# Seven half-depth products (Strassen) for queries, keys and gates of a linear-attention layer, over two halves of the tokens

## What is computed

```
h = layernorm(x)
qkv = silu(h @ qkv_w.T)            # 32 heads of 128; q, k, v per head
gate = sigmoid(h @ gate_w.T)       # 2048 x 4096
attn = causal linear attention with a decay per head (64 tokens, as one masked product)
y = gate * norm_w * rms_normalised(attn over all 4096)
x = x + y @ out_w.T
x = x + cross attention with ctx_4096 (64 channels, softmax over 512)
x = x + layernorm(x) @ identity.T
```

## Time and profile before

| | us |
|---|---|
| median of three runs | 2329.49 (2328.81 to 2329.71) |
| profiled execution | 2330.04 |
| its span, first to last instruction | 2328.2 |
| TensorE busy | 2291.6 (98%) |
| VectorE busy | 1208.5 (52%) |
| ScalarE busy | 732.1 (31%) |
| GpSimd busy | 442.3 (19%) |

### The profile page before, as it was taken

How to read it: one execution, slowest core, us unless ns; L and a number is a source line. 1 busy time by engine, 2 the same in 40 slices (tenths; PEclk the granted TensorE clock), 3 DMA queues, 4 the chain that set the end, 5 groups by cost and what they waited for, 6 DMA issues and landing times. The chain is left out here.

```text
span 2328.2 us, 34076 instructions
## 1 busy us (share of the span) xinstructions
PE 2291.6 (98%) x14112; PEld 1896.4 (81%) x14112; DVE 1208.5 (52%) x1493; ACT 732.1 (31%) x1303; POOL 442.3 (19%) x394
## 2 busy tenths in 40 slices
PE   8999999999999999999999999999999999799998
PEld 6888888888888888888888888888888888555555
DVE  6653545454444545454545454545444454576765
ACT  3232222232222222232323232223222222466664
POOL 2311122222211222222211122222211122211110
PEclk9999999999999999999999999999999999899999
DMA  4010100000000001010101000000000000201000
GB/s 138 1 47 1 38 8 28 18 28 18 28 18 19 27 0 46 0 46 0 46 0 46 0 28 18 28 18 28 18 28 18 18 23 1 104 19 34 31 24 19
DMA packets 24046, 61.75 MB, mean 27 GB/s; under 512 B 2880, under 2 KB 5440, under 8 KB 23872
## 3 DMA queue, kind: packets, MB, share of 16 engines
q1 hardware_dynamic: 24000, 61.11, 7.6%
HBM read 56.90 MB, written 4.19 MB: 26 GB/s over the span
## 5 line engine op out<-in xcount | busy, mean ns | idle before, releaser
L444 PE MATMUL bank<-xn_hi,w_hi 128*128 128x512 f32 x1536 | 612.2, 399 | 2.9 <-DVE w_lo L327 2.9
L446 PE MATMUL bank<-xn_hi,w_lo 128*128 128x512 f32 x1536 | 599.6, 390 | 0.0
L445 PE MATMUL bank<-xn_lo,w_hi 128*128 128x512 f32 x1536 | 599.2, 390 | 0.0
L220 POOL TENSOR_TENSOR sq<-attn 128x512 f32<-128x512 f32 x128 | 179.0, 1398 | 1527.8 <-ACT attn L289 1517.0
L444 PEld LDWEIGHTS bank<-xn_hi,w_hi 128*128 128x128 f32 x1536 | 288.9, 188 | 63.8 <-issue 3.2
L446 PEld LDWEIGHTS bank<-xn_hi,w_lo 128*128 128x128 f32 x1536 | 288.8, 188 | 61.6
L445 PEld LDWEIGHTS bank<-xn_lo,w_hi 128*128 128x128 f32 x1536 | 289.2, 188 | 55.6
L489 PE MATMUL bank<-w_hi,xn_lo 128*128 128x256 f32 x1024 | 289.2, 282 | 0.0
L487 PE MATMUL bank<-w_hi,xn_hi 128*128 128x256 f32 x1024 | 289.2, 282 | 0.0
L488 PE MATMUL bank<-w_lo,xn_hi 128*128 128x256 f32 x1024 | 289.0, 282 | 0.0
L363 DVE TENSOR_TENSOR qk<-bank,qk 128x512 f32<-128x512 f32 x256 | 174.0, 690 | 218.9 <-ACT qk L253 216.8
(11 more groups left out here) (89 smaller groups left out, 2709.5 us busy)
## 6 DMA issues: line engine op xcount, KB each, us to landing
raw<-w_qkv SPq DMA_DIRECT2D x48, 512.0 KB, 3.7
raw<-w_gate SPq DMA_DIRECT2D x16, 512.0 KB, 4.4
raw<-w_out SPq DMA_DIRECT2D x16, 512.0 KB, 3.2
stage<-ctx_in SPq DMA_DIRECT2D x16, 256.0 KB, 2.8
xr<-x SPq DMA_DIRECT2D x4, 1024.0 KB, 11.2
out<-attn_acc SPq DMA_DIRECT2D x16, 256.0 KB, 2.0
attn_acc<-x SPq DMA_DIRECT2D x3, 1024.0 KB, 7.8
attn_acc<-x SPq DMA_DIRECT2D x4, 256.0 KB, 3.9
```

Of the source, the lines that this page charges most:

```text
L220: nc.gpsimd.tensor_tensor(sq[:, :], attn[:, h], attn[:, h], ALU.mult).then_inc(sq_made, 1)
L444: nc.tensor.matmul(dst, hi, xn_hi[:, c, s], start=(c == 0), stop=False)
L445: nc.tensor.matmul(dst, hi, xn_lo[:, c, s], start=False, stop=False)
L446: i = nc.tensor.matmul(dst, weights(w_lo, w, c, h), xn_hi[:, c, s], start=False, stop=(c == CH - 1))
```

## The change

Queries, keys and gates are now made for a half of the tokens (1024, `half`) at a time and two row blocks at once, by Strassen's seven products with half the features each (2 chunks, so 6 matmuls; 42 for what were 48). The row blocks of a call are query and key of one head (`QK0`, `QK1`) or the gates of both heads (`GATE`). One pass of `body(half, g)` (called a unit; 32 of them) does the work of two steps. The loop over groups is run twice, once per half, and the weights of each group are loaded and cut in both.

- The sums of weight blocks (S1 to S4) are made by GpSimd in `mix`, four instructions of 256 columns per call; ScalarE and VectorE then cut seven blocks instead of four.
- The sums of token blocks (T1 to T4) are made once per half by GpSimd in `token_sums`, before they are turned, so 16 transposes are done for two tiles where eight were.
- Three of the products go into bank 2 (`CHAIN`), one into bank 3 (`SECOND`), two into bank 4 (`THIRD`). Between products ScalarE copies a bank out (`snapshot`), TensorE goes on adding to the bank, and VectorE adds the copy to another bank (`add_snapshot`). TensorE waits for these inside the call.
- One key block lies in SBUF, so its silu product is made by GpSimd (`keys_second`).
- The squares are made by ScalarE out of PSUM (`square`), the gated product is written over the weighed result in PSUM (`gated`), and `y_hi` and `y_lo` are cut from there. The copy `attn` is gone. GpSimd only adds.
- The output product of the second block of a unit is done in the next unit, the values of a unit half in the one before.
- In the second stage the turn of `xn3` and its cut move ahead of the fourth turn.

```diff
+        PRODUCTS = ((A11, B11, CHAIN, "first"), (A12, B21, SECOND, "only"), (S2, T2, CHAIN, "more"),
+                    (S1, T1, THIRD, "first"), (S3, T3, CHAIN, "more"), (S4, B22, THIRD, "last"),
+                    (A22, T4N, CHAIN, "last"))
...
@@ SyncE @@
+                def body(half, g):
+                    sp.wait_ge(w0_ready, count(half, g, 4, 2))
+                    load_pair(raw0, g, GATE, raw0_landed)
+                    sp.wait_ge(w1_ready, count(half, g, 2, 2))
+                    load_flat(w_out[g])
...
+                    sp.wait_ge(w0_ready, count(half, g, 4, 4))
+                    load_pair(raw0, nxt, QK0, raw0_landed)
+                    sp.wait_ge(wo_ready, count(half, g, 1, 1))
+                    load_flat(w_v[nxt])
+                    sp.wait_ge(scores_ready, count(half, g, 4, 4))
+                    sp.dma_start(decays[:, :, :], decay[:, bass.ds(nxt * HG, HG), :]).then_inc(decay_landed, 16)
+                    sp.wait_ge(wv_ready, count(half, g, 1, 2))
+                    load_pair(raw1, nxt, QK1, raw1_landed)
...
@@ GpSimd @@
+                def body(half, g):
+                    mix_gate(half, g)
+                    keys_second(half, g, 0)
+                    keys_second(half, g, 1)
+                    if not last:
+                        mix_qk0(half, g + 1)
+                    elif half == 0:
+                        mix_qk0(1, 0)
...
+                        token_sums(1, 0)
+                    squares(half, g)
+                    if not last:
+                        mix_qk1(half, g + 1)
+                    elif half == 0:
+                        token_sums(1, 1)
+                        mix_qk1(1, 0)
+                        token_sums(1, 2)
+                        token_sums(1, 3)
...
@@ ScalarE @@
+                def project_qk(half, g, call):
+                    snapshot(half, g, call, qk[:, 0, 0], 0)
+                    act.wait_ge(c_added, count(half, g, 9, 3 * call + 1))
+                    nc.scalar.activation(qk[:, 0, 0], bank[:, SECOND], ACT.Sigmoid).then_inc(c_sig, 1)
+                    snapshot(half, g, call, qk[:, 0, 1], 1)
+                    snapshot(half, g, call, qk[:, 1, 1], 2)
...
+                    nc.scalar.activation(sq[:, 0], qk[:, 1, 1], ACT.Sigmoid).then_inc(c_sig, 1)
...
+                    nc.scalar.activation(qk[:, 0, 1], bank[:, THIRD], ACT.Sigmoid).then_inc(c_sig, 1)
+                    act.wait_ge(p_mm, count(half, g, 21, 7 * call + 7))
+                    nc.scalar.activation(qk[:, 1, 0], bank[:, CHAIN], ACT.Sigmoid).then_inc(c_sig, 1)
...
@@ ScalarE @@
+                def body(half, g):
+                    y_high(half, g - 1, 1)
...
+                    project_qk(half, g, QK0)
+                    cut_gate(half, g)
+                    project_qk(half, g, QK1)
+                    cut_out(half, g)
+                        for j in (2, 3):
+                            v_sigmoid(half, g, j)
+                    project_gate(half, g, (half, g + 1) if not last else ((1, 0) if half == 0 else None))
+                    square(half, g, 0)
+                    y_high(half, g, 0)
+                    square(half, g, 1)
+                        cut_qk0(half, g + 1)
+                        for j in (0, 1):
+                            v_sigmoid(half, g + 1, j)
+                        cut_qk1(half, g + 1)
...
@@ VectorE @@
+                def body(half, g):
+                        y_low(*previous, 1)
+                    project_qk(half, g, QK0, lambda: cut_qk1(half, g, 0))
+                    cut_qk1(half, g, 1)
+                        add_out(*previous, 4)
+                    cut_gate(half, g, 0)
+                        add_out(*previous, 5)
+                    cut_gate(half, g, 1)
+                        add_out(*previous, 6)
+                        add_out(*previous, 7)
...
+                    decay_scores(half, g, 0)
+                    project_qk(half, g, QK1)
+                    cut_out(half, g)
...
@@ TensorE @@
+                def strassen(half, g, call, w_hi, w_lo, banks_free=None):
+                    for n, (a, b, to, part) in enumerate(PRODUCTS):
+                        if n == 2:
+                            pe.wait_ge(snapped, count(half, g, 9, 3 * call + 1))
+                        if n == 4:
+                            pe.wait_ge(snapped, count(half, g, 9, 3 * call + 2))
+                        if n == 5:
+                            pe.wait_ge(snapped, count(half, g, 9, 3 * call + 3))
+                        if n == 6:
+                            pe.wait_ge(c_added, count(half, g, 9, 3 * call + 2))
...
+                        for c in range(2):
...
@@ TensorE @@
+                def body(half, g):
...
+                        strassen(half, g, QK0, w0_hi, w0_lo, lambda: pe.wait_ge(v_ready, count(half, g, 4, 2)))
...
+                        for i in range(TT, HT):
+                            project_out(*previous, i)
...
+                    make_scores(half, g, 0)
+                    pe.wait_ge(w1_ready, count(half, g, 2, 2))
+                    strassen(half, g, QK1, w1_hi, w1_lo)
...
+                        for j in (2, 3):
+                            project_v(half, g, j)
+                    pe.wait_ge(scores_ready, count(half, g, 4, 2))
+                    make_scores(half, g, 1)
+                    pe.wait_ge(w0_ready, count(half, g, 4, 4))
+                    strassen(half, g, GATE, w0_hi, w0_lo)
...
+                    weigh(half, g, 0)
...
+                    weigh(half, g, 1)
+                    if not last:
...
+                        for j in (0, 1):
+                            project_v(half, g + 1, j)
...
+                        for i in range(TT):
+                            project_out(half, g, i)
+                    elif half == 0:
...
+                        turn(1, 0)
...
+                        project_out(half, g, 0)
+                        project_out(half, g, 1)
+                        turn(1, 1)
+                        for i in (2, 3):
...
+                            project_out(half, g, i)
+                        turn(1, 2)
+                        turn(1, 3)
...
+                        for j in (0, 1):
...
+                            project_v(1, 0, j)
...
@@ second stage, TensorE @@
-                    turn(t, 3)
                     if t:
...
                         turn_xn3(t - 1)
+                    turn(t, 3)
                     weigh(t, 2)
```

More of the change, by code:

```diff
@@ L30 @@
 TT = BT // P
+HT = 2 * TT
 EPS = 1e-5
@@ L190, in _ @@
+                for half in range(2):
+                    r = rolled(body, half)
+                    with nc.Fori(r.start, r.stop, engines=[sp.engine], hint_back_edge=True) as g:
+                        body(half, g)
+                    body(half, GROUPS - 1)
                 for t in range(2):
@@ L311, in _, with cut, cut_qk0 @@
-                for tb in range(TB):
-                    step(GROUPS - 1, tb, last=True)
+                def cut(dst, raw, part, done):
+                    s = slice(0, 4) if part == 0 else slice(4, 7)
+                    nc.scalar.activation(dst[:, s], raw[:, s], ACT.Copy).then_inc(done, 1)
+                def cut_qk0(half, g):
+                    for part in range(2):
+                        act.wait_ge(mixed0, count(half, g, 8, 4))
+                        cut(w0_hi, raw0, part, hi0_cut)
@@ L417, in _, with cut @@
[L417 to L429 removed]
+                def cut(dst, hi, raw, part, done):
+                    s = slice(0, 4) if part == 0 else slice(4, 7)
+                    nc.vector.tensor_tensor(dst[:, s], raw[:, s], hi[:, s].bitcast(F32), ALU.subtract).then_inc(done, 1)
@@ L523, in step, with weigh @@
+                def weigh(half, g, b):
                     for h in range(HG):
@@ L559, in _, with project_out @@
-                sums(range(TILES - TT, TILES))
+                def project_out(half, g, i):
+                    s = slice(i % TT * P, (i % TT + 1) * P)
+                    dst = bank[:, out_bank(half, g, i)]
+                    for h in range(HG):
+                        nc.tensor.matmul(dst, y_hi[:, h, s], wo_hi[:, h], start=(h == 0), stop=False)
+                        nc.tensor.matmul(dst, y_hi[:, h, s], wo_lo[:, h], start=False, stop=False)
+                        k = nc.tensor.matmul(dst, y_lo[:, h, s], wo_hi[:, h], start=False, stop=(h == HG - 1))
+                    k.then_inc(out_mm, 1)
@@ new lines, in _ @@
+                pe.wait_ge(const_landed, 16)
+                turn(0, 0)
+                turn(0, 1)
+                pe.wait_ge(wv_ready, 1)
+                project_v(0, 0, 0)
+                turn(0, 2)
+                project_v(0, 0, 1)
+                turn(0, 3)
+                project_v(0, 0, 2)
+                pe.wait_ge(x_ready, 14)
+                project_v(0, 0, 3)
+                for half in range(2):
+                    r = rolled(body, half)
```

(3 more changed lines are left out.)

932 lines of the change are left out of this document (544 added, 388 removed).

## The result

The changed kernel takes 2225.62 us (median; 2224.54 to 2226.27), against 2329.44 before: a ratio of 0.9554, 95% interval 0.9538 to 0.9571. That is 103.8 us less. The forecast was 2218 us in a range of 2198 to 2256. Its profiled execution took 2226.27 us, its span is 2224.5, the mean granted clock 0.994.

The account below looks back on a forecast made before the run. TensorE's stream bounds the kernel. First QK0 at 36.5, then 1825.5, 3.4, 17 and 6.2 end the attention stage at 1888.6, 110.9 us sooner; less 1 in the second stage, the forecast is 2218 us, range 2198 to 2256.

Parts of the forecast that it names:

- The cut: Steady attention units: 18 fewer matmuls take 4.15 us from each unit, leaving 57.41; 32 units save 132.7 us.
- The others keep pace: Inside Strassen calls: all four new waits stay hidden, by 0.5 us each, if ScalarE and VectorE reach their instructions in time.
- Rival 3: Strassen calls: ScalarE late to first snapshots exposes every call's handovers; 1.5 us lost per call gives 2362 us; 5%.
- The start: Before the first QK0 call: it begins at 36.5 us; the start costs 10 us, bounds 6 and 19.
- First unit: Scores directly behind QK0 and QK1, nothing between: two waits of 1.7 us each, 3.4 us.
- Between the halves: Change from half 0 to half 1: 16 us plus 1 for a lower clock, 17, between 10 and 28.
- End: End of the attention stage: last `y_high` waits for `out_mm`, 2.4 us, and two sums of 1.9; 6.2 us.
- Second stage: Earlier turn of `xn3` removes a wait, but `add_ffn` moves back: 1 us gained in all; bounds 7 gained, 5 lost.
- Lateness in the queues: Strassen calls: a snapshot or add reached late in some calls stalls TensorE 1 us per unit, 32 us, 2250; 18%.
- Cuts beside GpSimd: Between QK0 and QK1: three VectorE cuts meet GpSimd's work, 2.2 us per unit, 70 us, 2288; 8%.
- Slower than before, by late snapshots: Strassen calls: slower than before once ScalarE is 1.8 us late to each first snapshot; 5%.
- The halves cost less: Start and middle at their lower bounds, second stage at its gain: 4 + 7 + 6 us less, 2201; below 2200 6%.

Follow-up runs that it names:

- `eight_products`: The changed kernel with the last of the seven products computed twice, one more product per call: 2350.46 us.
- `late1`: The changed kernel with one more ScalarE copy of 512 columns ahead of each call's first snapshot: 2229.74 us.
- `late3`: The changed kernel with three more ScalarE copies ahead of each call's first snapshot: 2325.54 us.
- `gate_order`: The changed kernel with the gate call's second snapshot before the sigmoid, and the very first unit's cut of `w_v` behind the last snapshot: 2222.27 us.
- `old_xn3`: The changed kernel with the second stage's old order, `xn3` turned and split after the fourth turn: 2229.80 us.
- `pool_squares`: The changed kernel with only GpSimd's part of the old form: ScalarE copies the bank, GpSimd multiplies and adds; VectorE stays with the banks: 2313.55 us.
- `sbuf_y`: The changed kernel with the whole old form of squares and gated product, through SBUF instead of PSUM: 2375.75 us.
- `end_only`: The changed kernel with the last unit's second `y_hi` and `y_lo` in the buffers of w0, and sums ahead of the last output tile: 2217.41 us.
- `pool_busy`: The changed kernel with eight more GpSimd additions of 512 columns per unit, behind the first key product: 2227.49 us.

## Why the prediction was right, and where it was not

The total was 7.6 us low, inside the range. Against the sum made on the profiled execution (2218.1; measured 2226.27) it goes so:

- *The cut.* 4.15 us per unit, unit of 57.41: measured 57.47, and in `eight_products` 4.08 per unit. Over 29 units the 0.06 to 0.07 makes 1.9 us. Right.
- *The others keep pace.* No steady unit has a wait. The slack of 0.58 that I worked out is 0.57 between the rows and 0.39 in use (`late1`, `late3`). The 0.69 for writing a bank, the 0.60 for a square and the 0.81 for 256 columns were 0.70, 0.60 and 0.73. Right, but the layout left out one chain: GpSimd's squares, mix of QK1, ScalarE's cut, `y_hi`, first snapshot. It has 1.4 us of margin, and only because the squares have left GpSimd. Rival 3 names it (a cut that waits for GpSimd's mix), but no margin was worked out for it. I had costed "squares and gated product from PSUM" by the length of `y_lo` and a smaller load on GpSimd alone; that part is worth 2.7 us in the old kernel and 150 in the new one.
- *The start.* 36.5, measured 39.8: mis-sized by 3.3. The second pair of x tiles landed late (VectorE's statistics wait 2.77 until 8.49), and the layout had no transfers in it.
- *First unit.* The two waits for scores were 1.41 and 1.46, not 1.7 each. The wait for `w_v` was missing, though I had named the gate call as ScalarE's tight place: I checked it with the steady unit's times. Together 1.3 more.
- *Between the halves.* 17, measured 15.1, inside 10 to 28; `gate_order` shows that 1.4 of it was VectorE's statistics.
- *End.* The wait for `y_lo` was 2.07, not 2.4. An idle time of 1.2 in the last unit's QK0 call, which no wait in the trace explains, and the half clock behind the wait (1.5) were missing; with the small differences it is 2.8 more. The stage ends at 1896.0 instead of 1888.6.
- *Second stage.* 1 gained; measured 0.2, by luck of two terms. The order is worth 4.1 (`old_xn3`): the delay of `add_ffn` that I counted against it does not bind. And the stage's first 31 us took 4.6 longer than before. The clock was at 0.57 in the first 3.35 us, where the kernel before had 1.00, but that start alone doesn't decide it (see "The end of the stage"). The 0.45 per tile that I read for the wait for `xn3_lo` was 0.40: 6.0 us in 15 waits of the kernel before.

The total is nearer than its terms: the start, the first unit, the end, the steady units and the second stage were low by 3.3, 1.3, 2.8, 1.9 and 0.8, the change of halves was high by 1.9, and 8.2 is left.

The rivals. *Lateness in the queues* did not happen in the steady stream, and its price is known now: behind the first 0.39 us, what a first snapshot is late is lost in full, 96 times. *Cuts beside GpSimd*: the mechanism is there, and its price per unit was 1.0 where I had 2.9, and hidden: of three cuts one started first and lost nothing, and two found only 0.63 of an addition left. The Trainium skill, "SBUF — State Buffer", section "SBUF: two separate sides", says that the one that starts first has the shared ports for its whole instruction and the other stands still meanwhile. These rows agree to within 0.14 us: the later one loses what is left of the first, which is 0.63 here and 1.21 at 1073.87, and not a whole instruction each time, as I had priced it. Instructions with an operand in a bank kept 0.69 in both. *Slower than before, by late snapshots*: the mechanism is confirmed, and the point comes sooner than the 1.8 us late to each that I had put: 1.5 us late costs 100 us and all but cancels the change (0.39 of slack where I had 0.6, and 103.8 us to lose where I had 111), and `pool_squares` and `sbuf_y` show the way there, a cut that waits for GpSimd's mix. The first loss was some 2 us away: 1.4 ahead of `y_hi`, 0.3 behind it, 0.39 of slack. *The halves cost less* needed 6 us for the start and 10 for the middle; they cost 13.4 (39.8 - 11.6 - 14.8) and 15.1.

## What to carry to other kernels

Before costing an edit at "its engine has time", follow the queues it passes through: a load on an engine that is a third busy was worth 88 us, since one of its results, the mix, stood ahead of three instructions of ScalarE (cut, `y_hi`, snapshot) that TensorE's next wait needed. A part that is worth nothing in the old schedule (2.7 us) can be what the new one rests on (150 us), so try parts in both. Places outside the loop (start, first unit, change of halves, last unit) need a layout of their own: all but 2 us of the error of the attention stage came from there. When two engines share ports, the order of their starts prices the meeting: what starts first loses nothing, so a cost of "so much per meeting" is too coarse.

## What the runs showed of the hardware

- A stall of TensorE can cost more than itself. Behind waits of 0.9 us the granted clock stayed at 1.00 (`late3`). Behind 1.87 the windows have 0.76 and 0.67 in some units of `pool_squares`, and in others the clock stayed at 1.00; it also stayed behind 2.58 in some units of `sbuf_y`. Behind 4.1 it was 0.50 for some 6 us, which added 2.8. So the length of the wait alone doesn't tell it.
- The first 30 us of the second stage, the same code in all, took up to 6 us more or less, which goes with the clock granted there: at 0.50 for 6.8 us of the first 40 in `end_only`, for 17.1 in the changed kernel, for 23.9 in `sbuf_y`. The stage takes 322.6 to 329.1 us to the end, over the eleven kernels with the new order. What decides it stays open; the wait at the end of the first stage alone does not (`late1` and the changed kernel both have one of 2.1).
- VectorE writing to and reading from the same bank in place took as long as its other instructions of 512 columns with a bank: 0.70 us against 0.69.
- VectorE's cuts and GpSimd's instructions, both with all inputs in SBUF, don't slow each other down evenly: the later one is longer by what is left of the earlier, less 0.12 to 0.15 us. In `pool_busy` 156 instructions of GpSimd that start inside a cut show it, and in `pool_squares` 1.84 and 1.89 instead of 1.04 and 1.29, with 0.94 and 0.74 of a cut left.
